# Decoder, layer 0 cross attention: the softmax's exponentials taken head by head on ScalarE, with the maximum as bias and the sum taken along

## The reference, cut to what matters

```
def proj(x, W):
    return (x @ W.T).reshape(b, -1, HEADS, D_K).transpose(0, 2, 1, 3)
qh, kh, vh = (proj(q, Wq), proj(k, Wk), proj(v, Wv))
att = jnp.einsum('bhqd,bhkd->bhqk', qh, kh) / jnp.sqrt(jnp.float32(D_K))
att = jnp.where(mask, NEG, att)
att = jax.nn.softmax(att, axis=-1)
out = jnp.einsum('bhqk,bhkd->bhqd', att, vh)
out = out.transpose(0, 2, 1, 3).reshape(b, -1, D_MODEL)
return out @ Wo.T
```

## Time and profile before

| | |
|---|---|
| three runs | 2679.78, 2680.76, 2696.95 us |
| median | 2680.76 us |
| the profiled execution: its time | 2688.81 us |
| the profiled execution: its span, first to last instruction | 2687.1 us |
| the stage of the change | about 275 to 497 us of the span |
| granted TensorE clock, mean over the span | 0.916 |

### The profile page before, as it was taken

How to read it: one execution, slowest core, us unless ns; L and a number is a source line. 1 busy time by engine, 2 the same in 40 slices (tenths; PEclk the granted TensorE clock), 3 DMA queues, 4 the chain that set the end, 5 groups by cost and what they waited for, 6 DMA issues and landing times. The chain is left out here.

```text
span 2687.1 us, 35728 instructions
## 1 busy us (share of the span) xinstructions
PE 2288.1 (85%) x10898; PEld 1600.9 (60%) x10899; DVE 1182.4 (44%) x3373; ACT 675.3 (25%) x1301; POOL 610.0 (23%) x780
## 2 busy tenths in 40 slices
PE   5887788711999946888888878989999999999998
PEld 3555355610777734455555546776677777777776
DVE  2442798641333345666666534554322222222244
ACT  1211344200111122444444432211222212222221
POOL 1110577345000042333332220011700000000053
PEclk9998899755999976899988979978999999999999
DMA  6000000412122223333333300005411110010033
GB/s 221 0 0 20 1 1 1 173 53 86 61 64 62 65 60 85 74 80 78 82 76 72 64 18 4 5 32 201 166 37 31 33 34 31 31 35 31 26 94 98
DMA packets 122399, 160.46 MB, mean 60 GB/s; under 512 B 21106, under 2 KB 90546, under 8 KB 122034
## 3 DMA queue, kind: packets, MB, share of 16 engines
q1 hardware_dynamic: 110002, 125.53, 16.7%
q0 software_dynamic: 12288, 33.57, 3.9%
HBM read 75.68 MB, written 49.28 MB: 47 GB/s over the span
## 5 line engine op out<-in xcount | busy, mean ns | idle before, releaser
L1459 PE MATMUL e_up_ps<-e_wgu,e_xT 128*128 x1152 | 344.9, 452 | 0.0
L1565 DVE TENSOR_TENSOR e_h<-e_act_g,e_up_ps 128x344 f32<-128x344 f32 x208 | 106.7, 513 | 475.8 <-PE e_ht_ps L1466 438.5
L2049 DVE CUSTOM_DVE_ANT_0 a_s_ps<-a_s_ps,a_causal 128x512 f32<-128x512 f32 (+3 forms) x512 | 241.0, 515 | 122.8 <-PE a_s_ps L1834 121.9
L1459 PEld LDWEIGHTS e_up_ps<-e_wgu,e_xT 128*128 128x128 f32 x1152 | 218.9, 190 | 103.7
L1973 ACT ACTIVATE a_prob<-a_st_ps 128x512 f32<-128x512 f32 (+1 forms) x384 | 198.0, 523 | 302.3 <-PE a_st_ps L1851 299.7
L1492 ACT ACTIVATE e_act_g<-e_up_ps 128x344 f32<-128x344 f32 x208 | 95.2, 457 | 674.8 <-DVE e_h L1565 452.2
L1414 POOL DMA_INDIRECT e_wgu<-slots_y,slot x64 | 60.9, 952 | 657.3 <-DMA slots_y<-e_y 609.7
L1834 PE MATMUL a_s_ps<-a_ks,a_qs 68*128 68x512 f32 (+3 forms) x512 | 158.0, 376 | 59.5 <-DVE a_most L2049 46.2
L1851 PE MATMUL a_st_ps<-a_qs,a_ks 128*128 128x512 f32 (+3 forms) x512 | 188.8, 420 | 13.7 <-DMA a_qs<-a_m_lo 10.6
L1475 PE MATMUL e_y_ps<-e_wd,e_hT 128*128 x864 | 198.4, 379 | 0.0
L1740 POOL TENSOR_SCALAR_AFFINE_SELECT a_prob<-a_prob 128x256 f32<-128x256 f32 x256 | 101.1, 419 | 369.5 <-ACT a_prob L1973 369.3
(11 more groups left out here) (387 smaller groups left out, 3800.2 us busy)
## 6 DMA issues: line engine op xcount, KB each, us to landing
e_xin<-slots_x SPq DMA_DIRECT2D x144, 128.0 KB, 2.0
slots_y<-e_y SPq DMA_DIRECT2D x144, 128.0 KB, 1.7
slots_x<-zero_row SPq DMA_DIRECT2D x1, 9216.0 KB, 27.0
e_w<-in_L_ffn_w SPq DMA_DIRECT2D x16, 512.0 KB, 9.9
a_qs<-a_hi SPq DMA_DIRECT2D x32, 256.0 KB, 5.2
a_ks<-a_hi SPq DMA_DIRECT2D x32, 256.0 KB, 5.1
a_qs<-a_lo SPq DMA_DIRECT2D x32, 256.0 KB, 6.4
a_ks<-a_lo SPq DMA_DIRECT2D x32, 256.0 KB, 7.0
```

Source lines behind the costliest of these rows:

```text
L1459: last = pe.matmul(up_ps[:, 2 * half_ + u_, 0:H], xT[:, j, k * P:(k + 1) * P], up[:, k, u_, half_ * H:(half_ + 1) * H], start=k == 0, stop ...
L1565: dve.tensor_tensor(h[:, half_ * H:(half_ + 1) * H], act_g[:, :], up_ps[:, 2 * half_ + 1, 0:H], ALU.mult).then_inc(h_kept, 1)
L2049: last = dve.tensor_tensor_reduce(s_ps[:, u % 2, off:off + cols], s_ps[:, u % 2, off:off + cols], causal[:, S - cols:], 1.0, -3.0e38, ALU. ...
```

## The change

`subtract` is gone from POOL's loop, and the sum over the keys from DVE's `shares`. `maximum` writes the negated maximum. `exponentials` is a loop over the 16 heads: each is an ACTIVATE over 64 columns that takes the head's negated maximum as its bias (exp(x - max)) and gives the sum of its results along (`accum_out`) into `total`. It waits for `max_done` in place of `less_max`, and for `share_done` of the tile four before, which read the same slot of `total`; `maximum` waits for `exp_done` of the tile four before in place of `less_max`. Nothing else moves.

```
-            def subtract(i):
-                pool.wait_ge(max_done, i + 1)
-                pool.tensor_tensor(heads(i), heads(i), most[:, i % RING].unsqueeze(2).broadcast_to([P, HEADS, SC]),
-                                   ALU.subtract).then_inc(less_max, 1)
...
             def exponentials(i):
-                act.wait_ge(less_max, i + 1)
-                act.activation(prob[:, i % RING, :], prob[:, i % RING, :], ACT.Exp).then_inc(exp_done, 1)
+                act.wait_ge(max_done, i + 1)
+                after(act, share_done, i + 1 - RING)
+                for h in range(HEADS):
+                    step = act.activation(heads(i)[:, h], heads(i)[:, h], ACT.Exp, bias=most[:, i % RING, h:h + 1],
+                                          accum_out=total[:, i % RING, h:h + 1])
+                step.then_inc(exp_done, 1)
...
             def maximum(i):
                 dve.wait_ge(capped, i + 1)
-                after(dve, less_max, i + 1 - RING)
-                dve.tensor_reduce(most[:, i % RING], heads(i), AX.X, ALU.max).then_inc(max_done, 1)
+                after(dve, exp_done, i + 1 - RING)
+                dve.tensor_reduce(most[:, i % RING], heads(i), AX.X, ALU.max, negate=True).then_inc(max_done, 1)
             def shares(i):
                 dve.wait_ge(exp_done, i + 1)
-                dve.tensor_reduce(total[:, i % RING], heads(i), AX.X, ALU.add).then_inc(sum_done, 1)
-                dve.wait_ge(sum_done, i + 1)
                 after(dve, prob_done, i + 1 - RING)
                 dve.reciprocal(share[:, i % RING], total[:, i % RING]).then_inc(share_done, 1)
```

More of the change, by code:

```diff
@@ L472, in l0_cross_attention @@
         q_done, q_kept, v_done, v_kept = sem("q_done"), sem("q_kept"), sem("v_done"), sem("v_kept")
-        s_done, capped, max_done, less_max = sem("s_done"), sem("capped"), sem("max_done"), sem("less_max")
-        exp_done, sum_done, share_done, prob_done = sem("exp_done"), sem("sum_done"), sem("share_done"), sem("prob_done")
+        s_done, capped, max_done = sem("s_done"), sem("capped"), sem("max_done")
+        exp_done, share_done, prob_done = sem("exp_done"), sem("share_done"), sem("prob_done")
         p_turned, p_kept = sem("p_turned"), sem("p_kept")
@@ L534, in _ @@
             for i in range(STEPS):
-                if tile(i):
-                    subtract(i)
                 if tile(i - 1):
```

## The result

The changed kernel takes 2731.56 us (median of 4 runs, 2726.29 to 2735.96) against 2684.0 us for the kernel before (4 runs, 2679.78 to 2696.95). The ratio is **1.0168, 95% interval 1.0126 to 1.021**, so it is slower by about 45 us. 2728 us were forecast, with 2692 to 2805 as the range. The profiled execution has a span of 2732.0 us against 2687.1.

What follows compares the result with a forecast made beforehand. PE and DVE were taken to set the pace at 25.5 us a sequence, ACT after the change at 31.2. Eight sequences make 45.6 us, plus 2 at the end: +47.6 on 2680.76 gives 2728 us, range 2692 to 2805.

Steps and rivals of the forecast that it cites:

- A read is an ordinary short instruction on ACT: On ACT, each of 512 accumulator reads overlaps as other short instructions do and adds 0.094 us; this forecast had chance 0.50.
- DVE's hidden read: On DVE the accumulator read after a maximum hides, r = 0; the prediction declined to take this zero for ACT.
- E = 5.47 us: On ACT, one tile's sixteen exponentials: 3.96 us without sums plus 16 reads of 0.094 us, against 1.05 us before.
- 9.3 + 4 E: ACT's cost of a four-tile sequence: 7.38 us other work, 1.93 us unfillable waits, four tiles' exponentials; 31.2 us predicted.
- +5.7 a sequence, 45.6, and 2 for the end: Over the stage: 5.7 us above 25.5 a sequence, 45.6 us for eight, 2 us at the end, sum +47.6 us.
- the cancelling at the start: In the slower first sequences ACT has more room, but the pipeline's fill grows by an E; the two were let cancel.
- DVE waits for ACT: DVE's `shares` would idle about 4 us, waiting for ACT's last head, in steps without the norm.
- The bank's round trip: ACT's 1.75 us wait before `keep_query`, through one bank begun by ACT's own copy; exponentials behind it cannot fill it.
- POOL's and DVE's relief is worth nothing: Removing POOL's 1.90 us a tile shortens only hidden latency; DVE's 1.21 us brings little, with PE's 22.4 us right behind.
- ACT becomes the bound when its sequence passes 25.5 us: ACT's sequence cost would set the pace above 25.5 us, reached at 4.05 us of exponentials a tile.
- the free read: Rival on ACT: a read costs under 0.04 us, ACT's sequence 25.1 us at zero, time 2680 to 2708; chance 0.18.
- TensorE's clock: Rival on PE: its clock falls, growing round trip and short transposes by 1 to 2 us a sequence, 2740; chance 0.04.

Runs made afterwards that it cites:

- e1: The changed kernel with all sums left out, biased exponentials kept: pace 25.8 us, stage 230.7 us, ratio 1.0036 against the kernel before.
- e4: The changed kernel with sums taken along for heads 0 to 7 only, the others left out: pace 27.6 us, stage 249.0 us, ratio 1.0109 against the kernel before.
- e6: The changed kernel with ACT's exponentials ahead of the second half of transposed rows and queries: pace 30.3 and 32.0 us, ratio 1.0223 against the kernel before.
- e7: The kernel before with DVE's sums left out: pace 24.4 us, stage 218.1 us, ratio 0.9984 against the kernel before.
- e5: The kernel before, POOL's subtraction kept, exponentials by head without bias, sums along on ACT: pace 26.9 and 28.4 us, ratio 1.0029 against the kernel before.
- e8: The kernel before with exponentials only cut into heads, subtraction on POOL and sums on DVE: pace 26.9 and 28.4 us, ratio 1.0056 against the kernel before.
- e10: The changed kernel with DVE's norm work moved ahead of the reciprocal: pace 30.8 to 31.0 us, stage 272.5 us, ratio 1.0187 against the kernel before.
- e2: The changed kernel with the sums back on DVE, bias still on ACT: pace 28.3 us, stage 249.0 us, ratio 1.0077 against the kernel before.
- e9: The changed kernel with sums back on DVE and DVE's norm work ahead of the sum: pace 25.2 us, stage 230.9 us, ratio 1.0041 against the kernel before.

## Why the prediction was right, point by point

- **A read is an ordinary short instruction on ACT, 0.094 us in its step.** Right: 0.09 by the timeline, 0.082 by the stages of e1 and the change, 0.098 by the paces of e4 and the change, where ACT is the bound in both. The record is 0.193 us long and overlaps like others. DVE's hidden read the earlier trace rows was no guide, as assumed.
- **E = 5.47 us and ACT's sequence 9.3 + 4 E = 31.2.** Measured 5.41 (from a tile's first head to the end of its last read in the timeline) and 30.76. The parts err against each other: other work is 28.15 - 4 x 5.41 = 6.5 us, since records overlap, in place of 7.38, and the waits are 2.6 in place of 1.93. That the sum is only 0.4 us off is in part luck.
- **+5.7 a sequence, 45.6, and 2 for the end.** The seven periods between the eight sequences grew by 38.0 us together, the rest of the stage by 9.8. Sum 47.8 against 47.6. The split is off: by the forecast seven periods were 39.9 us and the rest 7.7. The periods were priced 1.9 us too high, and the fill and the end 2.1 us too low, since the cancelling at the start was not exact. That the two errors cancel is luck; the forecast was good to about 2 us and not to 0.2.
- **DVE waits for ACT, about 4 us in steps without the norm.** Right: 4.6 us there, and 0.7 in the two steps that come behind norm work. The bank's round trip stays, 1.9 us. Right, and e6's order did not fill it.
- **POOL's and DVE's relief is worth nothing.** Not as it was argued. e7 puts DVE's at 6.8 us of stage if ACT had stayed as it was, and e5 against e1 puts POOL's at 1.1 us a sequence. Four buffers and the steps of distance don't hide the latency: e8 lengthened the exponentials by 1.4 us a tile, and a sequence grew by 1.4. Under an ACT that is the bound the relief does not show, as e10 shows for DVE: its busy time fell from 17.8 to 15.9 us and the stage by 0.2.
- **ACT becomes the bound when its sequence passes 25.5 us.** This step failed, though the forecast did not rest on it. e8 with ACT at 17.4 us and e2 at 22.8 are paced 26.9 and 28.3. The sum over one engine's work is a lower bound; between it and the truth stood the loop through `add_to_x` and `keep_weighted`, of which e9 took a part away. For the free read I had allowed up to 1 us a sequence for this, and e1's pace is 0.7 above ACT's 25.1.
- **TensorE's clock.** I gave it 0.04. The event came all the same: the granted clock fell from 1.00 to 0.94 in every steady sequence of the change, and PE's busy time rose from 22.4 to 24.0 us. What that cost is not measured, since no sequence of the change ran at 1.00. ACT's waits for PE are 0.7 us a sequence above the 1.93 that I counted; if they would else have stayed as they were, that is the most it cost, where the rival had 1 to 2. Elsewhere a sequence at 0.94 or 0.95 lasts longer than one at 1.00 by 1.5 us in e5 and e8, 0.9 in e3 and 1.6 in e6; in e2 one at 0.92 is only 0.2 longer.

## What to carry to other kernels

Count the instructions, not the elements, when work is cut so that an engine can take a bias or a sum along: 64 columns cost 0.066 us within one wide ACTIVATE here, and alone 0.146 for themselves, 0.09 for a bias and 0.09 for the read of the accumulator. A step sum of one engine gives the size of a change when that engine ends up bound; while it is not, look at which wait stands in front of which queued work, since moving the norm's work ahead of a waiting instruction was worth 18 us of stage in e2, part of it through less contention with GpSimd. And look at what an instruction starts on GpSimd: what VectorE does next may stand still beside it, as the `tensor_scalar` rows did and the reductions did not.

## What the runs showed of the hardware that was not expected

- On ACT, a bias from a tensor and a read of the accumulator each add 0.09 us to the step of a short ACTIVATE (0.146, 0.24, 0.24, 0.33), although the read's record lasts 0.19 us.
- Four float32 `tensor_scalar` rows of 256 columns on DVE take 1.38 us alone, 1.84 with 0.7 us of a GpSimd `tensor_tensor` beside them, 2.90 when that starts just ahead, 4.00 beside two of them in a row (e5, e7).
- With PE busy 24.0 of 30.76 us its granted clock was 0.94 in each steady sequence of the change. In e6 it was 1.00 in four of seven periods (PE busy 22.8 of 30.3) and 0.89 to 0.95 in the others; why one and not the other stays open.
